# A graph layer and an expert layer on one core: distances on turned node blocks, list factors of one-input operations, rows fetched ahead of weights

## The reference

```python
x = x + gnn(layernorm(x), r, W, y, edge_index)
x = x + ffn(layernorm(x))

def gnn(mems, r, W, y, edge_index):          # mems [12500, 256]
    mems2 = mems.at[yi].set(r[0])
    d2 = jnp.sum(jnp.square(mems2 - r), axis=-1)
    _, nbr = jax.lax.top_k(-d2, 7)           # 7 nearest nodes of r, joined to node yi
    deg = segment_sum(w, col) + 2.0
    dinv = rsqrt(deg)
    out = segment_sum((dinv[row] * w * dinv[col])[:, None] * (mems2 @ W)[row], col)
    return out + (2.0 * dinv * dinv)[:, None] * (mems2 @ W)

def ffn(h, gate_w, gate_b, w1, b1, w2, b2):  # 8 experts, capacity 1954 rows each
    probs = softmax(h @ gate_w + gate_b); idx = argmax(probs)
    pos = rank of the token within its expert
    buf[idx, pos] = h                        # kept where pos < capacity
    y = relu(buf @ w1 + b1) @ w2 + b2        # per expert
    return y[idx, pos] * prob * kept
```

## Time and profile before

| | us |
|---|---|
| median of 3 runs | 2591.44 (2588.29 to 2591.5) |
| the profiled execution's own time | 2592.29 |
| its span, first to last instruction | 2590.8 |
| first to last gather of the loop | 247.0 to 1807.6 |
| first product of the experts | 1873.6 |

### The profile page before, as it was taken

The page is one execution under the profiler, slowest core; times in us unless marked ns, Lnnn a source line. Parts: engine busy times, 40 slices in busy tenths (PEclk is TensorE's granted clock), DMA queues, the critical chain, the costliest instruction groups (busy, mean ns, idle before and its releaser), DMA issues. The chain is left out here.

```text
span 2590.8 us, 36610 instructions
## 1 busy us (share of the span) xinstructions
PE 1964.7 (76%) x11096; PEld 1697.6 (66%) x11096; DVE 1318.2 (51%) x3683; ACT 1011.5 (39%) x1769; POOL 1548.2 (60%) x1612
## 2 busy tenths in 40 slices
PE   2002777866786796786878888998599999999995
PEld 1002655855675585675767788887488788788875
DVE  7969875255325425335242257776444444454443
ACT  1377555345425525435343133333232323322332
POOL 6631777777777777777777777776223422422234
PEclk8555888988898898898989999999699999999998
DMA  9216433743473474573756777777512212212121
GB/s 264 66 57 181 120 103 115 259 136 104 152 253 106 128 254 128 165 240 104 238 166 206 229 213 208 210 208 173 143 33 71 83 36 71 76 36 71 42 68 28
DMA packets 235522, 359.05 MB, mean 139 GB/s; under 512 B 46585, under 2 KB 172697, under 8 KB 235221
## 3 DMA queue, kind: packets, MB, share of 16 engines
q0 software_dynamic: 74176, 194.10, 26.3%
q1 hardware_dynamic: 159860, 160.86, 20.2%
q10 hardware_dynamic: 1312, 2.10, 0.3%
HBM read 305.38 MB, written 56.40 MB: 140 GB/s over the span
## 5 line engine op out<-in xcount | busy, mean ns | idle before, releaser
L669 POOL DMA_INDIRECT arena<-z_table,arena x1216 | 1185.4, 975 | 462.0 <-issue 361.6
L1776 PE MATMUL bank<-arena 128*128 128x128 f32 x4864 | 711.0, 307 | 267.2 <-DMA arena<-z_table,arena 143.4
L1776 PEld LDWEIGHTS bank<-arena 128*128 128x128 f32 x4864 | 662.1, 218 | 364.3 <-issue 293.1
L1248 DVE TENSOR_TENSOR nodes<-nodes,bank 128x256 f32 x304 | 128.1, 421 | 755.8 <-PE bank L1776 740.8
L729 POOL DMA_INDIRECT out<-arena x128 | 130.7, 1021 | 419.1 <-DVE arena L1660 396.6
L2017 PE MATMUL bank<-arena 128*128 128x256 f32 (+1 forms) x1472 | 330.2, 384 | 14.2 <-DVE arena L1608 8.9
L927 ACT ACTIVATE nodes<-bank,arena 128x256 f32<-128x256 f32 (+1 forms) x368 | 152.7, 466 | 457.5 <-PE bank L2017 457.5
L2029 PE MATMUL bank<-arena,nodes 128*128 128x256 f32 (+1 forms) x1472 | 326.0, 379 | 0.0
L2017 PEld LDWEIGHTS bank<-arena 128*128 128x128 f32 x1472 | 282.7, 196 | 55.1 <-DVE arena L1608 10.9
L817 ACT ACTIVATE arena<-iota_h,arena 128x490 f16<-128x490 f16 x280 | 194.6, 695 | 304.3 <-PE bank L1788 304.3
L2029 PEld LDWEIGHTS bank<-arena,nodes 128*128 128x128 f32 (+1 forms) x1472 | 272.6, 187 | 40.1 <-issue 1.0
(11 more groups left out here) (315 smaller groups left out, 1850.8 us busy)
## 6 DMA issues: line engine op xcount, KB each, us to landing
arena<-z_table SPq DMA_DIRECT2D x96, 768.0 KB, 4.6
arena<-z_table,arena POOLq DMA_INDIRECT x1216
arena<-in_L_ffn_w SPq DMA_DIRECT2D x14, 1024.0 KB, 7.0
z_table<-nodes SPq DMA_DIRECT2D x14, 896.0 KB, 6.7
x_rows<-nodes SPq DMA_DIRECT2D x98, 128.0 KB
arena<-in_x SPq DMA_DIRECT2D x48, 256.0 KB, 3.1
out<-nodes SPq DMA_DIRECT2D x96, 128.0 KB
nodes<-in_x SPq DMA_DIRECT2D x12, 896.0 KB, 11.5
```

Source lines behind the costliest of these rows:

```text
L669: nc.gpsimd.indirect_dma_start(gath[:, slot, t, :], None, z_table, bass.IndirectOffsetOnAxis(ap=src_idx[:, tile_at:tile_at + 1], axis=0)). ...
L1776: last = nc.tensor.matmul(agg_bank[i][:, k * P:(k + 1) * P], gath[:, i, t, k * P:(k + 1) * P], sel[:, i, t, :], start=(t == 0), stop=(t == ...
```

## The change

Distances: PE turns blocks of 4 windows (25 blocks) into PSUM so that features lie on partitions, ACT takes the square of turned block plus `-r` (`far_squares`, two operations of 512 columns per block), and PE sums over the features by products with a column of ones, one per window and half, into `dist_bank`. `differ`, ACT's block square and DVE's `sum_squares` go. The squares use three buffers, the turned blocks two. DVE normalises all 98 windows, and does the means, variances and normalising ahead of the bounds of the edge groups; PE spreads the bounds between two of its blocks (after block 20). ACT counts 6 batches before it waits for the variances, and takes four blocks of squares behind each later batch. ACT scales chunks 2 and 5 of `z`, DVE the other five. The loop no longer waits for the distances.

List factors: each window's two matrices come from one operation each, with one tensor input and scalars per partition; the two factors per unit go, two or three operations on one column per window come instead.

Experts: SP waits for the first four gathers, then issues `b2_rows` and the second expert's weights; PE reads its nine counts before the list is ready, ACT and DVE read theirs as they come to need them, ACT after its first `norm_rows`.

```diff
-    ACT_WIN = 40
-    EARLY = 9
+    EARLY = 6
+    NBK = -(-NW // 4)
+    SQ = 3
+    SPREAD_AT = 20
+    Z_ACT = (2, 5)
+    Z_DVE = [c for c in range(NZC) if c not in Z_ACT]
...
+        dist_bank = bank[7]
+        far_bank = [(bank[2], bank[3]), (bank[0], bank[6])]
...
@@ sync
             sp.wait_ge(S["list_ps"], NLB)
+            sp.wait_ge(S["fixed"], 1)
+            for slot in range(2):
+                sp.wait_ge(S[f"xs_in{slot}"], 32)
+            sp.dma_start(b2_rows, ...).then_inc(S["w_small"], 16)
             load_weights(1, 1)
-            sp.wait_ge(S["fixed"], 1)
-            sp.dma_start(b2_rows, ...).then_inc(S["w_small"], 16)
@@ gpsimd
-            pool.wait_ge(S["dist_ok"], 2 * NZC)
@@ scalar
+            def far_squares(b):
+                wide = P * min(4, NW - 4 * b)
+                act.wait_ge(S["nT_ps"], b + 1)
+                if b >= SQ:
+                    act.wait_ge(S["dist_ps"], b - SQ + 1)
+                for k in range(KD):
+                    nc.scalar.activation(squares[b % SQ][:, k, 0:wide], far_bank[b % 2][k][:, 0:wide], ACT.Square,
+                                         bias=neg_r[:, k:k + 1]).then_inc(S["square_ok"], 1)
...
             for b in range(EARLY, 2 * NZC):
-                for w in range((b - EARLY) * part, min((b - EARLY + 1) * part, ACT_WIN)):
-                    normalise(w)
                 count_first(b)
+                for n in range(4 * (b - EARLY), min(4 * (b - EARLY + 1), NBK)):
+                    far_squares(n)
...
-            for b in range(2 * NZC):
-                act.wait_ge(S["diff_ok"], KD * (b + 1))
-                nc.scalar.activation(diff[:, b % DR, :, :, :], diff[:, b % DR, :, :, :], ACT.Square).then_inc(S["square_ok"], 1)
-                if b % 4 == 3:
-                    ... chunk b // 2 scaled by dinv
+            act.wait_ge(S["deg_ok"], 2)
+            for c in Z_ACT:
+                ... chunk c scaled by dinv
@@ vector
             for w in range(NW):
+                nc.vector.tensor_scalar(nodes[:, :, w, :], nodes[:, :, w, :], rstd[:, w:w + 1], shift[:, w:w + 1],
+                                        ALU.mult, ALU.add).then_inc(S["mem_ok"], 1)
...
+            dve.wait_ge(S["mem_ok"], NW)
+            dve.wait_ge(S["nT_ps"], NBK)
...
-            def differ(b): ...
-            def sum_squares(b): ...
+            for c in Z_DVE:
+                for k in range(KD):
                     rows = nodes[:, k, c * ZC:(c + 1) * ZC, :]
                     ins = nc.vector.tensor_tensor(rows, rows, dinv[...], ALU.mult)
+                ins.then_inc(S["z_ok"], 1)
...
-                nc.vector.tensor_tensor(list_lo[:, i % LB, :, :], iota_r..., pos_lo..., ALU.is_equal).then_inc(S["list_in"], 1)
-                nc.vector.tensor_tensor(list_hi[:, i % LB, :, :, :], unit_row..., unit_tile..., ALU.mult).then_inc(S["list_in"], 1)
+                for t in range(LW):
+                    nc.vector.tensor_scalar(list_lo[:, i % LB, t, :], iota_r[:, :], pos_lo[:, w + t:w + t + 1], None, ALU.is_equal)
+                    nc.vector.tensor_scalar(list_hi[:, i % LB, t, :, :]..., iota_r[:, 0:NE * CT],
+                                            pos_hi[:, w + t:w + t + 1], kept[:, w + t:w + t + 1],
+                                            ALU.is_equal, ALU.mult).then_inc(S["list_in"], 1)
@@ tensor
+            def turn_nodes(b):
+                pe.wait_ge(S["mem_ok"], min(4 * (b + 1), NW))
+                if b >= 2:
+                    pe.wait_ge(S["square_ok"], KD * (b - 1))
+                for k in range(KD):
+                    for i in range(min(4, NW - 4 * b)):
+                        last = nc.tensor.transpose(far_bank[b % 2][k][:, i * P:(i + 1) * P], nodes[:, k, 4 * b + i, :], ident[:, :])
+                last.then_inc(S["nT_ps"], 1)
+            def sum_squares(b):
+                pe.wait_ge(S["square_ok"], KD * (b + 1))
+                for i in range(min(4, NW - 4 * b)):
+                    for k in range(KD):
+                        last = nc.tensor.matmul(dist_bank[:, 4 * b + i:4 * b + i + 1], squares[b % SQ][:, k, i * P:(i + 1) * P],
+                                                ones[:, 0:1], start=(k == 0), stop=(k == KD - 1))
+                last.then_inc(S["dist_ps"], 1)
+            for b in range(NBK):
+                turn_nodes(b)
+                if b == SPREAD_AT:
+                    spread_bases()
+                if b:
+                    sum_squares(b - 1)
+            sum_squares(NBK - 1)
...
+            all_took = [pe.value_load(taken_i[0:1, i:i + 1], ...) for i in range(NE + 1)]
             pe.wait_ge(S["list_ok"], 1)
...
-            turn_or_skip(0, 0, pe.value_load(taken_i[0:1, 0:1], ...))
-            all_took = [pe.value_load(taken_i[0:1, i:i + 1], ...) for i in range(NE + 1)]
+            turn_or_skip(0, 0, all_took[0])
```

More of the change, by code:

```diff
@@ L319, in build @@
         stage_f2 = carve([EB, P])
-        at[0] = here - EB * P
+        at[0] = 0
         cross_row = carve([TILES])[0:1, :]
+        squares = []
+        for begins in (here - EB * P, here, here + 16 * P // 2 + U * P):
+            at[0] = begins
+            squares.append(carve([KD, 4 * P]))
+        assert at[0] <= here + (2 * 16 * (P + NW)) // 2
         at[0] = here + 16 * P // 2
@@ L922, in _ @@
                             act.sem_inc(S["tick"], 1)
-                        with act.If(took[j] > CHUNKS[c][0]):
+                        with act.If(all_took[q * 2 + j] > CHUNKS[c][0]):
                             act.wait_ge(S["l2_ps"], q * (2 * PC) + (2 * s + 2))
@@ new lines, in _ @@
+            then(nc.vector.tensor_scalar(r_y[:, :], r_rows[:, :], mine_y[:, 0:1], None, ALU.mult))
+            then(nc.vector.tensor_scalar(invalid[:, :], node_id[:, :], float(N), -3.0e38, ALU.is_ge, ALU.mult))
+            then(nc.vector.tensor_scalar(tok_id[:, :], node_id[:, :], 1.0, None, ALU.add))
+            then(nc.vector.memset(taken_i[:, :], 0))
+            for c in range(NZC):
+                dve.wait_ge(chunk_moved[c], LOADED[c])
+                for w in range(c * ZC, (c + 1) * ZC):
+                    nc.vector.bn_stats(bn1[:, w, :], nodes[:, :, w, :]).then_inc(S["bn1_ok"], 1)
@@ new lines, in _ @@
+            then(nc.vector.tensor_scalar(gap2[:, :], gap2[:, :], -0.5, 1.5, ALU.mult, ALU.add))
+            then(nc.vector.tensor_tensor(gap2[:, :], gap2[:, :], not_y[:, :], ALU.mult))
+            then(nc.vector.tensor_tensor(rstd[:, :], rstd[:, :], gap2[:, :], ALU.mult))
+            nc.vector.tensor_tensor(shift[:, :], rstd[:, :], neg_mean[:, :], ALU.mult).then_inc(S["shift_ok"], 1)
+            dve.wait_ge(S["shift_ok"], 1)
+            for w in range(NW):
+                nc.vector.tensor_scalar(nodes[:, :, w, :], nodes[:, :, w, :], rstd[:, w:w + 1], shift[:, w:w + 1],
+                                        ALU.mult, ALU.add).then_inc(S["mem_ok"], 1)
@@ L1071, in _ @@
[L1071 to L1080, removed]
@@ L1094, in _ @@
[L1094 to L1101, removed]
@@ L1107, in _ @@
             dve.wait_ge(S["mem_patched"], KD)
[L1109 to L1118, removed]
-            def sum_squares(b):
-                dve.wait_ge(S["square_ok"], b + 1)
-                nc.vector.tensor_reduce(dist[:, b * U:(b + 1) * U], diff[:, b % DR, :, :, :], AX.XY, ALU.add).then_inc(S["dist_ok"], 1)
             dve.wait_ge(S["less_ok"], NW)
@@ L1592, in _ @@
             dve.sem_inc(S["fixed"], 1)
+            then(nc.vector.memset(gate_l, 0.0))
+            dve.sem_inc(S["gate_in"], 1)
             dve.wait_ge(S["list_ps"], NLB)
@@ L1597, in _ @@
             dve.sem_inc(S["list_ok"], 1)
-            then(nc.vector.memset(gate_l, 0.0))
-            dve.sem_inc(S["gate_in"], 1)
             def feats(q, s, took):
@@ new lines, in sum_squares @@
+            def sum_squares(b):
+                pe.wait_ge(S["square_ok"], KD * (b + 1))
+                for i in range(min(4, NW - 4 * b)):
+                    w = 4 * b + i
+                    for k in range(KD):
+                        last = nc.tensor.matmul(dist_bank[:, w:w + 1], squares[b % SQ][:, k, i * P:(i + 1) * P], ones[:, 0:1],
+                                                start=(k == 0), stop=(k == KD - 1))
+                last.then_inc(S["dist_ps"], 1)
+            pe.wait_ge(S["edges_out"], len(EDGE_TURNS))
@@ L2031, in down @@
                     last.then_inc(S["l2_ps"], 1)
+            all_took = [pe.value_load(taken_i[0:1, i:i + 1], min_val=0, max_val=N) for i in range(NE + 1)]
             pe.wait_ge(S["list_ok"], 1)
```

159 lines of the change are left out of this document (75 added, 84 removed).

## The result

The changed kernel takes 2601.11 us (median of 6 runs, 2597.95 to 2602.96) against 2590.79 for the kernel before in the same job: a ratio of 1.0034, 95% interval 1.0022 to 1.0046, so slower, by little but clear of noise, where I forecast 2554.2 and a range of 2541 to 2582. The profiled execution took 2600.66, with a span of 2598.8; the one before had 2590.8. In the changed kernel the loop's gathers are L676, the gathers of expert rows L725, the turns L1730, the products with a column of ones L1738, ACT's squares L767, the scaling by `dinv` L1180.

What follows compares the result with a forecast made beforehand. POOL's gathers bound the loop, so its beginning, set by `dinv` and the stores of `z`, decides: 2592.3 - 24.5 (head) - 4 (list) - 8.7 (experts) = 2555.1, less 0.85 to the median: 2554.2 us, range 2541 to 2582.

Steps and rivals of the forecast that it cites:

- What bounds the kernel: Whole loop: POOL's gathers are the bound, so the loop's end moves with its beginning, which the head decides.
- When `dinv` is there: Head before the loop: PE's turned blocks are the bound, putting `dinv` at 176 us, for 171.1 before.
- the upper prices: PE's blocks at the upper clock: 2.7 us each, 25 blocks 68 us; at the lower clock 5.3 each.
- The row of turns alone: Earlier trace, evidence against the lower clock: with nothing but turns on PE, the clock rose from 0.50 to 1.00.
- The rival that came true: PE stays at 1.2 GHz through the blocks: 5.3 us each, `dinv` at 235, time 2613; chance 0.14.
- the lower bound of 2540.5: Fast end of the forecast's own range: `dinv` at 170, all of the list, shortest landing; rounded to 2541.
- From `dinv` to the loop: Stores of `z` are the bound: first gather at 227.8, 17th at 247.5 for 272.01; 24.5 us gained.
- The list: Loop's gathers beside list operations: removing two-input operations gains 4 us, between 12.0 and nothing, or a loss of 12.
- The third I took: Share of the 12.0 us excess over 273 late gathers taken as gain from the new list factors: 4 us.
- The experts: Experts' beginning: rows landing sooner 4.1 us, PE's reads moved earlier 4.6; together 8.7, between 4.6 and 9.3.
- My rival: Experts and list give only PE's reads, rows landing as late as now: time 2562; chance 0.12.
- now lie ahead of the list: Experts' beginning: PE's reads of counts, 4.6 us before its first product, move under the wait for rows.

## Why the prediction was wrong

**What bounds the kernel:** right. In every kernel above the end follows the first gather of the loop, and that follows `dinv` by 51.6 to 52.1 us with the new head.

**When `dinv` is there:** this is the step that failed. I took "the upper prices", 2.7 us a block, because turns alone had raised the clock before and PE has no pauses between blocks. The price itself was right (2.6 measured at 1.00, 5.01 at 0.50 for my 5.3), its clock was not: two blocks ran wholly at the upper one, some 22 at the lower, and `dinv` came at 217.8 for 176. With 64 columns, where the clock holds, `dinv` is at 169.7 and the time 2550.7, inside the range. The error is thus one of the choice between two prices that both stood on paper. The row of turns alone didn't cover a block whose turns take only a third of its time, and I read "hardly a pause" as a reason for the upper clock: the blocks had none and were granted 0.50. The rival that came true had 0.14; its 2613 was too high by 12, as `dinv` came 17 earlier than the 235 it assumed (5.0 per block for 5.3, and the first blocks faster), while the stages behind `dinv` gave some 3.4 less than it took (0.7 before the 17th gather, 0.8 on the list's chain, 1.3 and 0.9 in the experts, less 0.3 in the loop); the other 1.7 lie in how the profiled executions stand to their spans and medians. Two small slips beside it: a turn takes 0.11 at the upper clock (8 in 0.91 us) and not 0.10, as the 30 in 3.00 count turns that the window cuts, and the lower bound of 2540.5 leaves out the 0.85 that the other sums take off.

The Trainium skill has a rule that lies near: "TensorE: Matmul & The Clock Gate", "Why this matters for your kernels", advises for matmuls with M (the rows of the result) below 512 to run all tiles of K before the next DMA or to pad M, since the clock otherwise goes up and down. Its case is another one: here PE waited for no DMA, and what was thin was the operand that streams, with one column. Padding that operand helped all the same, with 64 columns (1.00) and not with 16 (0.50).

**From `dinv` to the loop:** right, stage by stage (51.6 for 51.8; 20.6 for 19.7). The stores were the bound, not the scaling.

**The list:** 4.3 in the loop for a forecast of 4, in part by luck. The factors do act on the gathers (977 ns for 1009 and 1011); that it is their second tensor input isn't shown, as the new operations are also half as wide and the two per unit are gone. The third I took was low: over the 273 late gathers 32 ns are 8.7 of the 12, and from the first gather to the loop's end the factors alone gave 6.7 (1560.7 to 1554.0). The middle of the loop, which varies by some 4 us, hid the rest in the changed kernel. On the chain I took nothing, and 0.8 was lost.

**The experts:** 7.4 for 8.7. The rows land sooner than I took (2.7 for 3.3), as the run with PE's signals ahead shows; in the changed kernel ACT doesn't start by them. (My rival took 3.3 for the most that other landings need; in the earlier trace rows it is the median.) What failed is that PE's reads "now lie ahead of the list": in the program they do, on the chip they begin at 1871.6, with the list, last 5.9 us, and in the changed kernel hold back ACT's first normalising as well. Why they begin 2.8 us behind the end of PE's last list product (1868.84) no run here tells.

## What to carry to other kernels

Where work is moved to TensorE, price it at both clocks, and don't take the busy share for the clock: here products of one column filled the busy time and the clock fell to 0.50, and then the turns beside them took almost twice as long too (8 in 1.74 us for 0.91). Columns that are computed and thrown away can be free (64 for one: 1.90 for 1.84 to 1.95 us) and buy the clock back, which was worth 47 us here; then look for the next wait, since a faster engine runs into what was hidden (3.1 us for the bounds). An instruction that is moved ahead in the program doesn't run ahead unless its engine gets to it earlier.

## What was not expected of the hardware

Useless work made the kernel faster: 196 extra turns saved some 24 us (one execution). The same blocks can run at either level: those with doubled turns ran at 1.00 from 98 to 169 us and, once down, stayed at 0.50 to their end, 25 us later; why is open. It isn't so for every block: the interleaved ones with 64 columns fell behind a wait and came back to 1.00 within some 10 us. And the order of the same instructions counts at either clock: a turn and a product by turns took 2.3 us per block for 2.6, and 4.3 for 5.0.
